# Expert tiles that gather their own token rows by slot lists and add into DRAM, in place of a dispatch stage

## The reference, cut to what matters

```python
edge_index = jnp.stack([src, dst])
xn = _layernorm(x, axis=-1)                                   # x: 6250 x 256, 100000 edges
x = x + gnn(xn, edge_index, ...) + mix(xn[None], ...)[0]      # two graph attention layers; linear attention
x = x + ffn(_layernorm(x, axis=-1)[None], ...)[0]

def ffn(x, gate_w, gate_b, w1, b1, w2, b2, gamma, beta):      # 16 experts, 256 -> 512 -> 256
    topk_vals, topk_idx = jax.lax.top_k(x @ gate_w + gate_b, 2)
    topk_w = jax.nn.softmax(topk_vals, axis=-1)
    h = jax.nn.relu(jnp.einsum('bsh,ehf->bsef', x, w1) + b1)
    expert_out = jnp.einsum('bsef,efh->bseh', h, w2) + b2
    sel = jnp.take_along_axis(expert_out, topk_idx[:, :, :, None], axis=2)
    y = x + jnp.sum(topk_w[..., None] * sel, axis=2)
    return (y - mean(y)) / jnp.sqrt(var(y) + 1e-5) * gamma + beta
```

## Time and profile before

| | us |
|---|---|
| median of 3 runs | 3250.85 (3249.6 to 3253.1) |
| the profiled execution | 3245.28 |
| its span, first to last instruction | 3243.4 |
| mean granted TensorE clock | 0.817 |

### The profile page before, as it was taken

The page is one execution under the profiler, slowest core; times in us unless marked ns, Lnnn a source line. Parts: engine busy times, 40 slices in busy tenths (PEclk is TensorE's granted clock), DMA queues, the critical chain, the costliest instruction groups (busy, mean ns, idle before and its releaser), DMA issues. The chain is left out here.

```text
span 3243.4 us, 51573 instructions
## 1 busy us (share of the span) xinstructions
PE 2010.8 (62%) x11139; PEld 1632.5 (50%) x11140; DVE 1836.5 (57%) x5366; ACT 1005.1 (31%) x1903; POOL 1859.4 (57%) x2040
## 2 busy tenths in 40 slices
PE   1837777777777767456666555666670069999600
PEld 0525555555555545345544444545550059999500
DVE  3656666666666653655555555555694024444366
ACT  0524444444444425222222222222130023333222
POOL 0357777777777730777777777777562721111254
PEclk9968888888888888778787888787895579999855
DMA  2734444444444434344444444443466422222265
GB/s 55 223 87 128 127 126 126 126 127 127 126 126 126 126 107 171 91 107 107 107 107 107 107 107 107 107 106 107 144 204 194 155 71 70 70 70 71 70 186 178
DMA packets 266807, 387.84 MB, mean 120 GB/s; under 512 B 85081, under 2 KB 200539, under 8 KB 266609
## 3 DMA queue, kind: packets, MB, share of 16 engines
q0 software_dynamic: 92832, 255.84, 28.5%
q1 hardware_dynamic: 133093, 86.81, 9.5%
q10 hardware_dynamic: 40828, 44.59, 4.0%
HBM read 305.91 MB, written 81.54 MB: 119 GB/s over the span
## 5 line engine op out<-in xcount | busy, mean ns | idle before, releaser
L821 POOL DMA_INDIRECT gathered<-table,idx x1568 | 1499.0, 956 | 625.1 <-issue 497.1
L968 PE MATMUL psA_e<-gathered,hotf 128*128 128x260 f32 x3136 | 962.1, 474 | 11.9 <-DVE gathered L863 11.8
L968 PEld LDWEIGHTS psA_e<-gathered,hotf 128*128 128x128 f32 x3136 | 749.1, 245 | 160.9 <-issue 12.7
L960 PE MATMUL psT<-identb,hot 128*128 128x128 bf16 x1568 | 163.4, 267 | 672.6 <-DVE hot L846 672.6
L863 DVE TENSOR_TENSOR gathered<-gathered,psW_e 128x2048 f32<-128x2048 f32 x196 | 448.2, 2287 | 75.4 <-ACT psW_e L927 75.4
L960 PEld LDWEIGHTS psT<-identb,hot 128*128 128x128 bf16 x1568 | 120.5, 120 | 688.6 <-issue 608.9
L918 ACT ACTIVATE hotf<-hot 128x1024 f32<-128x1024 bf16 x196 | 207.1, 1057 | 765.0 <-DVE hot L846 764.8
L857 DVE TENSOR_TENSOR z_e<-both_e,gathered 128x32 f32<-128x32 f32 x196 | 37.7, 192 | 589.2 <-DMA gathered<-table,idx 589.2
L846 DVE TENSOR_SCALAR hot<-iota,code_r 128x128 bf16<-128x128 bf16 x1568 | 302.4, 287 | 2.2 <-issue 1.2
L1553 POOL DMA_DIRECT2D ys_d<-xo x113 | 61.1, 541 | 381.0 <-DVE xo L1513 381.0
L1493 ACT ACTIVATE w1e<-w 128x1024 f32 x113 | 119.5, 1058 | 409.7 <-PE xpsH L1534 265.0
(11 more groups left out here) (248 smaller groups left out, 2629.9 us busy)
## 6 DMA issues: line engine op xcount, KB each, us to landing
gathered<-table,idx POOLq DMA_INDIRECT x1568
w<-in_L_ffn_w ACTq DMA_DIRECT2D x8, 2048.0 KB, 16.0
xx<-xs_d SPq DMA_DIRECT2D x113, 128.0 KB, 2.0
ys_d<-xo POOLq DMA_DIRECT2D x113, 128.0 KB, 2.0
xs_d<-zero_rows SPq DMA_DIRECT2D x49, 256.0 KB, 2.9
table<-acc POOLq DMA_DIRECT2D x49, 130.0 KB
table<-acc SPq DMA_DIRECT2D x49, 130.0 KB, 1.9
xnT_d<-xnT ACTq DMA_DIRECT2D x49, 128.0 KB, 1.8
```

Of the source, the lines that this page charges most:

```text
L821: pool.indirect_dma_start(out=G[:, q, k, :], out_offset=None, in_=table, in_offset=bass.IndirectOffsetOnAxis(ap=idx[:, q, k:k + 1], axis=0 ...
L960: ins = pe.transpose(psT[:, k, :], hot[:, q, k, :], identb[:])
L968: ins = pe.matmul(psA[:, par, 0:GW], hotf[:, q, k, :], G[:, q, k, :], start=(k == 0), stop=(k == KT - 1))
```

## The change

The zero stores, `xs_d`, `ys_d`, `y_d` and the dispatch stage are gone. `combine` stores xf twice, to `xf_d` and to `moe_d`, each with one more tile of rows, and writes y + beta over `acc` in SBUF, where finish reads it. `order` goes on to make, for every slot of the 113 tiles, the row number `token` and the weight `weight`: for each tile of rows and each of the two choices, a one-hot matrix of the slot in its tile (128 x 128) is multiplied with a one-hot matrix of the tile number, once scaled by the row number (VectorE) and once by the share (GpSimd), and the products are summed in PSUM. Slots that nobody uses point at rows past the 6250.

`experts` gathers x from `xf_d` by `token` (GpSimd), loads the tile's row of b2 (SP), scales the result by `weight` (ACT) and adds it to `moe_d` by an indirect transfer that sums at its target (GpSimd). Each of these waits for the one before to land. `finish` loads `moe_d` eight tiles ahead, has no gathers or sums, and stores the output from GpSimd's queue.

```diff
 def combine(nc, a, xnT_d, xf_d, moe_d, ident, eps, acc, mixM, hot, share, sem):
-                if later(i, BUFS):
-                    pool.wait_ge(s[f"stored{q}"], (i - q) * 4)
-                pool.tensor_tensor(yb[:, q, :], y[:, q, :], beta[:], ALU.add).then_inc(s["yb"], 1)
+                pool.tensor_tensor(acc[:, ds(i, 1), 0:C].rearrange("p o f -> p (o f)"), y[:, q, :], beta[:], ALU.add).then_inc(s["yb"], 1)
...
-                act.wait_ge(s["yb"], i + 1)
-                act.dma_start(y_d[ds(i * P, P), :], yb[:, q, :]).then_inc(s[f"stored{q}"], 16)
                 act.wait_ge(s["xf"], i + 1)
                 act.dma_start(xf_d[ds(i * P, P), :], xf[:, q, :]).then_inc(s[f"xf_out{q}"], 16)
+                act.dma_start(moe_d[ds(i * P, P), :], xf[:, q, :]).then_inc(s[f"xf_out{q}"], 16)
 def order(nc, a, ident, ones, hot, share, token, weight, expert, w1e, w2, b1T, weights_in, sem):
...
+            def shares(i, q):
+                if later(i, 2):
+                    pool.wait_ge(s["listed"], i - 1)
+                for k in range(2):
+                    pool.tensor_scalar(at_tile[:, q % 2, k, 1, :], across[:, 0:XT], tile[:, ds(i, 1), k:k + 1].rearrange("p o f -> p (o f)"),
+                                       share[:, ds(i, 1), k:k + 1].rearrange("p o f -> p (o f)"), ALU.is_equal, ALU.mult).then_inc(s["shares"], 1)
...
+            def tokens(i, q):
+                if later(i, 2):
+                    dve.wait_ge(s["listed"], i - 1)
+                for k in range(2):
+                    dve.tensor_scalar(at_slot[:, q % 2, k, :], across[:], slot[:, ds(i, 1), k:k + 1].rearrange("p o f -> p (o f)"), None, ALU.is_equal)
+                    dve.tensor_scalar(at_tile[:, q % 2, k, 0, :], across[:, 0:XT], tile[:, ds(i, 1), k:k + 1].rearrange("p o f -> p (o f)"),
+                                      number[:, ds(i, 1)], ALU.is_equal, ALU.mult).then_inc(s["tokens"], 1)
+            tiles(dve, (0, tokens))
...
+                for k in range(2):
+                    ins = pe.matmul(psL[:, 0:2 * XT], at_slot[0:r, q % 2, k, :], at_tile[0:r, q % 2, k, :, :].rearrange("p a f -> p (a f)"),
+                                    start=(not later(i, 1) and k == 0), stop=(r == LAST and k == 1), skip_group_check=True)
+                ins.then_inc(s["listed"], 1)
 def experts(nc, a, xf_d, moe_d, ident, expert, token, weight, w1, w1e, w2, b1T, acc, weights_in, sem):
...
-                sp.dma_start(x[:, q, :], xs_d[ds(j * P, P), :]).then_inc(s[f"x{q}"], 16)
-            pairs(sp, (0, load))
+                sp.dma_start(b2[:, q % 2, :], a["L0_ffn_b2"][ds(e, 1), :].to_broadcast([P, C])).then_inc(s[f"b2_{q % 2}"], 16)
+            pairs(sp, (0, bias))
...
+            def scale(j, q):
+                act.wait_ge(s["o"], j + 1)
+                if later(j, 2):
+                    act.wait_ge(s["summed"], (j - 1) * 16)
+                act.activation(scaled[:, q % 2, :], o[:, q % 2, 0:C], ACT.Copy, scale=weight[:, ds(j, 1)]).then_inc(s["scaled"], 1)
+            pairs(act, (0, weights), (0, turned), (3, scale))
...
+            def number(j, q):
+                if later(j, BUFS):
+                    hold(dve, s["turned"], j - BUFS + 1, s["tick"])
+                dve.tensor_copy(source[:, q:q + 1], token[:, ds(j, 1)]).then_inc(s["source"], 1)
+
+            def number_again(j, q):
+                if later(j, 2):
+                    hold(dve, s["summed"], (j - 1) * 16, s["tick"])
+                dve.tensor_copy(target[:, q % 2:q % 2 + 1], token[:, ds(j, 1)]).then_inc(s["target"], 1)
...
-            pairs(dve, (3, result), (1, relu))
+            pairs(dve, (0, number), (3, number_again), (3, result), (1, relu))
...
-                pool.dma_start(ys_d[ds(j * P, P), :], o[:, q, :]).then_inc(s[f"st{q}"], 16)
-            pairs(pool, (0, store))
+            def gather(j, q):
+                hold(pool, s["source"], j + 1, s["tick"])
+                pool.indirect_dma_start(out=x[:, q, :], out_offset=None, in_=xf_d,
+                                        in_offset=bass.IndirectOffsetOnAxis(ap=source[:, q:q + 1], axis=0)).then_inc(s[f"x{q}"], 16)
+
+            def add(j, q):
+                pool.wait_ge(s["scaled"], j + 1)
+                if later(j, 1):
+                    pool.wait_ge(s["summed"], j * 16)
+                hold(pool, s["target"], j + 1, s["tick"])
+                pool.indirect_dma_start(out=moe_d, out_offset=bass.IndirectOffsetOnAxis(ap=target[:, q % 2:q % 2 + 1], axis=0),
+                                        in_=scaled[:, q % 2, :], in_offset=None, compute_op=ALU.add).then_inc(s["summed"], 16)
+            pairs(pool, (0, gather), (3, add))
 def finish(nc, a, moe_d, out, eps, acc, sem):
...
+            deep(sp, (0, load))
+            deep(pool, (0, store))
+            deep(act, (3, unit_rows), (1, root))
-            tiles(dve, (3, add_second), (6, times_gamma), (3, stats), (2, add_first), (3, moments), (7, add_y), (4, invert), (0, number), (4, shift))
+            deep(dve, (1, moments), (4, times_gamma), (0, stats), (2, invert), (2, shift), (5, add_y))
```

More of the change, by code:

```diff
@@ L212, in build, with prepare_edges @@
             stage(gat_edges, 1, srcp, table[1], *edges, None)
-            stage(combine, a, xnT_d, y_d, xf_d, ident, eps, acc, mixM, hot, share)
+            stage(combine, a, xnT_d, xf_d, moe_d, ident, eps, acc, mixM, hot, share)
         with ExitStack() as ffn:
             w2 = sb("w2", [P, NX, FF // P, C], F32, ffn)
-            stage(order, a, ones, hot, place, expert, w2, weights_in)
             b1T = sb("b1T", [P, NX, FF // P], F32, ffn)
[L218 to L221, removed]
+            stage(order, a, ident, ones, hot, share, token, weight, expert, w1e, w2, b1T, weights_in)
+            stage(experts, a, xf_d, moe_d, ident, expert, token, weight, w1, w1e, w2, b1T, acc, weights_in)
+        stage(finish, a, moe_d, out, eps, acc)
     nc.clear_and_free_semaphores([weights_in])
-def prepare_edges(nc, a, srcp, ident, identb, ones, zero, iota, eps, code, lower, upper, first_tile, passes, sem):
+def prepare_edges(nc, a, srcp, ident, identb, ones, iota, eps, code, lower, upper, first_tile, passes, sem):
     with ExitStack() as ctx:
@@ L1092, in _, with combine @@
             tiles(pe, (0, turn), (1, project))
-def combine(nc, a, xnT_d, y_d, xf_d, ident, eps, acc, mixM, hot, share, sem):
+def combine(nc, a, xnT_d, xf_d, moe_d, ident, eps, acc, mixM, hot, share, sem):
     with ExitStack() as ctx:
@@ L1376, in _ @@
-            chain.link(dve.tensor_tensor(past[:], numbers[:].rearrange("o (t e) -> o t e", e=1).to_broadcast([1, XT, NX]),
+                chain.link(dve.tensor_tensor(picked, rank, hot[:, :, k, :], ALU.mult))
+                chain.link(dve.tensor_reduce(row[:, :, k], picked, AX.X, ALU.add))
+            chain.link(dve.tensor_copy(row_i[:], row[:]))
+            chain.link(dve.tensor_scalar(part_i[:], row_i[:], 7, None, ALU.arith_shift_right))
+            chain.link(dve.tensor_copy(tile[:], part_i[:]))
@@ L1448, in experts @@
+            tiles(pe, (0, lists))
+def experts(nc, a, xf_d, moe_d, ident, expert, token, weight, w1, w1e, w2, b1T, acc, weights_in, sem):
     with ExitStack() as ctx:
@@ L1550, in _, with finish @@
         def _(pool):
-            def store(j, q):
-                pool.wait_ge(s["o"], j + 1)
-                pool.dma_start(ys_d[ds(j * P, P), :], o[:, q, :]).then_inc(s[f"st{q}"], 16)
-            pairs(pool, (0, store))
-            for q in range(BUFS):
-                pool.wait_ge(s[f"st{q}"], 16 * uses(q, XT))
-def finish(nc, a, y_d, xf_d, ys_d, out, eps, place, share, sem):
+            def gather(j, q):
[10 more added lines that the diff above has]
+            pairs(pool, (0, gather), (3, add))
+            pool.wait_ge(s["summed"], 16 * XT)
+def finish(nc, a, moe_d, out, eps, acc, sem):
     with ExitStack() as ctx:
@@ L1617, in unit_rows @@
                     act.wait_ge(s["scaled"], i - BUFS + 1)
[L1618 to L1626 removed]
+                act.activation(unit[:, q % BUFS, :], moe[:, q, :], ACT.Identity, bias=rs[:, q % BUFS, 2:3], scale=rs[:, q % BUFS, 1:2]).then_inc(s["unit"], 1)
```

310 lines of the change are left out of this document (132 added, 178 removed).

## The result

The changed kernel takes 4006.4 us (median of 4 runs, 4004.8 to 4007.6), the kernel before 3252.0 beside it (3249.6 to 3254.2): 1.232 times as long, 95% interval 1.230 to 1.234. The forecast was 3872 us, with a range of 3680 to 4110.

What follows compares the result with a forecast made beforehand. No engine was busy over 62% of the span, so each stage had its own limit. 3245.3 + 796 (experts) - 90 (order, dispatch) - 85 (finish) = 3866, with 5.6 for the median 3872 us; range 3680 to 4110.

Steps and rivals of the forecast that it cites:

- The ring: Experts: turn, up, relu, row-number copy, gather, next turn wait in sequence; 10.74 us a tile instead of 3.73, stage +796 us.
- The rival that the rows come in time: Experts: gathers issued ahead or their wait covered, so a tile keeps 3.73 us and the total is 3080 us; 4%.
- The clock: Experts: TensorE's stall lowers its granted clock, costing 1.7 us a round on top of 9.04.
- the 4.04 us from the earlier trace: Experts: time from turn's start to relu's start behind up, read from the profile of the kernel before.
- The branch that was given 69%: Experts: the forecast itself, a 9.04 us round plus a clock loss of about 1 to 2.5 us a tile; 69%.
- the rival of a clock that stays low: Experts: all of a round's TensorE work at half clock, 12.77 us a round, total 4101 us; 8%.
- The adds: Experts: summing transfers, some 5.4 us to land, are covered by TensorE's stall; without it they would set about 6 us.
- that rival: Experts: adds take longer than a round or hold up the next gather in their queue; round 13.2 us, total 4150; 9%.
- Order, the wrong engine: Order: VectorE's four compares set 1.13 us a tile, 57 us added to 28; with dispatch gone, -90 us.
- Finish: Finish: gathers and weighted sums go; 1.5 us a tile, 96 us instead of 181, -85 us.
- the 15 us put behind the last VectorE instruction: End of finish: store, landing, barrier and a 9.3 us drain of GpSimd's queue, where it was 5 us before.
- Nothing for combine and the layers: Combine and graph layers: removing the zero stores gives 0; combine 0, with a bound of 0 to -8 us.

Runs made afterwards that it cites:

- no add: Changed kernel with the summing indirect DMA replaced by an increment of its semaphore, so experts contribute nothing to the output: 3985.7 us.
- stall filled: Changed kernel with eight spare 128x256 matmuls, thrown away, at the end of each of TensorE's rounds in experts: 3833.3 us.
- one round of lead: Changed kernel with loop offsets in experts altered so that row numbers and gathers run one round ahead of everything else: 3395.9 us.
- the run that scatters without summing: Changed kernel with row numbers and gathers two rounds ahead, and `compute_op=ALU.add` left out of the scatter: 3087.4 us.
- two rounds of lead: Changed kernel with only loop offsets in experts altered: row numbers, gather and b2 load run two rounds ahead: 3237.9 us, 0.995 of the kernel before.

## Why the prediction was right in kind and 134 us short

The forecast was made against the profiled execution, so its terms are compared there: experts 1235 forecast and 1357 found (+122), order 85 and 107 (+22), finish 96 and 81 (-15), and the stages ahead of order 0 and +12. Together that is the 141 us between 3866 and 4006.9.

**The ring, right.** The step that a tile's number stands behind the relu of the tile before, so that four buffers don't help, held: 113 of 113 turns wait for the gather, no add holds one up (no add: 0.06 us a tile), and offsets alone give back 768 us. The rival that the rows come in time never applied.

**Its length, the mis-sized term.** Means over 105 rounds from the timelines of the changed kernel, and over 104 of the one with the stall filled:

| part | forecast | changed kernel | stall filled |
|---|---|---|---|
| turn to relu, clock loss included | 4.04 + 1.7 | 7.06 | 5.25 |
| relu to the copy's start | 1.13 | 1.06 | 1.06 |
| copy's start to gather | 0.95 | 1.03 | 1.14 |
| gather to turn | 2.92 | 2.84 | 2.87 |
| round | 10.74 | 11.99 | 10.31 |

The latencies taken from finish and gat_edges were good to 0.1 us. The estimate of 2.3 us by the Trainium skill's page DMA: Bandwidth & Descriptors, section "Anatomy of one DMA — SWDGE (gpsimd) path", would have been 0.5 too short beside the 2.84 measured.

The clock was right in kind and somewhat dearer than put. From down to up these rounds take 3.48 us where the earlier trace rows have 1.73, and from up to relu 2.51 for 2.09: 2.2 us lost, where 1.7 were taken. The run with the stall filled says the same: its rounds have a median of 4.99 us from turn to relu (the 5.25 above is a mean at a clock of 0.96), 2.1 less than 7.06. The Trainium skill's page TensorE: Matmul & The Clock Gate, section "HAM oscillation — how this bites in real kernels", on matmuls between waits, agrees in direction: 0.71 with the stall and 0.96 with it filled.

The failing term is the 4.04 us from the earlier trace rows. There turn, down and up follow one another without a gap, and down starts 0.22 us after turn. Behind a stalled turn it starts 1.08 us after it (1.04 with the stall filled, so it isn't the clock).

The run with one round of lead settles that it comes from the stall: of its turns, in one and the same program, 55 waited for a gather and have down 1.17 us behind them on average, and the 55 between them waited for nothing and have it 0.22 us behind, every one. The traces show 0.29 to 0.67 us of issue in the gap (42.3 us in all in the changed kernel, have none), where TensorE comes to down's register load and waits only after the turn. And it counts from the landing of the rows: in the run that scatters without summing TensorE has hardly any idle time before its turns, and yet, by the landing times that its trace has for 56 gathers, down starts 0.50 us behind turn where the rows landed 0.91 us before turn, 0.37 where 1.04 and 0.28 where 1.12, which is 1.4 us from landing to down each time; where they landed 1.2 us before or earlier it is 0.22 (one of the 56 fits neither). So work that needs the landing first is hidden when rows come early. That it is just this register load and wait is argued and not shown.

The gap is 0.86 of the 1.25 us missing in these rounds, the clock about 0.45, and the other parts cancel to within 0.1. Over the whole stage, with its short first rounds, the turns are 11.83 us apart, 1.09 more than forecast, which is the 122 us.

None of the rivals priced this gap. The branch that was given 69%, a clock loss of up to 2.5 us, ended at 9.04 + 2.5 = 11.5 us a round, and 11.83 were found. The range held because it reached up to the rival of a clock that stays low (12.77 a round, 4101 us), and that rival did not come true: 2.2 us of clock were lost and not 3.73. That the time lies inside the range is in part luck.

**The adds.** Forecast: covered by the stall, and about 6 us each once the stall is gone. Found: covered, and 5.00 with two rounds of lead (issue 1.58, landing 2.8 to 2.9 after it, hand-over 0.6). From the start of its issue to its landing the summing transfer takes 4.4 us where 5.4 was put. Its issue alone is 1.58 us, a plain scatter's 0.98. The other half of that rival, that adds hold up gathers in the same queue, is false in the changed kernel (0.06 us a tile), and becomes true with lead, as the gathers of 3.3 to 4.0 us show.

**Order, the wrong engine.** The step took VectorE's four operations, 1.13 us, as the pace, and GpSimd's two for 0.8. They take 0.81 each, 1.62 together: 128x113 with a compare and a product costs as much as the 128x256 addition of the earlier trace rows, so half the columns didn't mean half the time. Without them order is 20 us shorter, which is nearly the whole miss of 22. VectorE's four took 2 x 0.370 + 2 x 0.353 = 1.45 us and not 1.13 either, beside GpSimd's; with GpSimd idle they take 2 x 0.341 + 2 x 0.287 = 1.26.

**Finish.** 1.5 us a tile was put and 1.35 found (bn_stats starts from 3927.4 to 3992.3, 48 intervals). Of the 15 us put behind the last VectorE instruction 8.2 came, because the drain took 4.05 us and not 9.3.

**Nothing for combine and the layers.** Combine took 141 us for 143, as put. It began 15 us late, and order 12, behind layers in which a gather takes 953 ns for 946. But in nine traces of kernels with the same code up to there order began between 2447 and 2465 us. So the 12 us are no cost of the change that these runs can show, and the removed stores of zeros gave nothing.

## What to carry to other kernels

When an index comes out of one engine's in-order loop, follow a round backwards on every engine in it, and count how many tiles the ring covers; buffers give no lead that the program order doesn't. Here offsets turned 1.23 times the time into 0.995, and one table for each parity of the tiles into 0.959. Price a ring with the gaps of an engine that has just been stalled, not with those of one that runs back to back, and check the repair for the next ring (here the adds, then a store in a load's queue).

## What the hardware showed that I had not expected

- A GpSimd indirect DMA that sums takes 1.58 us to issue and 4.4 from there to landing, a plain gather of the same rows 0.99 and 2.8. With adds in flight a gather's 2.8 grow to 3.3 and up to 4.0 (medians).
- The matmuls behind two stalled transposes start 1.0 to 1.2 us after them on average, and 0.22 us after two that didn't stall, in one and the same program.
- GpSimd's compare-and-multiply of 128x113 takes 0.81 us, its addition of two 128x256 tiles 0.79.
- VectorE's comparisons of 128x128 with one SBUF tile as input take 0.35 us while GpSimd works and 0.29 while it is idle; its bn_stats of 128x256, with one input as well, keeps its 0.42.
- VectorE's operations with two SBUF inputs take 0.08 to 0.13 us longer on average while GpSimd adds.
- Eight useless matmuls in each stall raised the granted clock from 0.71 to 0.96 and saved 173 us.
- On one chip the two layers took some 430 us longer in all four traces, and the kernel before, without a trace there, was 451 us slower. What was different is open.
